# Two chained layers on one Trainium2 core: one constant load moves from ScalarE's queue to GpSimd's, ten start-up products instead of twelve, and batch 1's first products in another order

## The chip, the cores and the metric

The kernel runs on one core of a Trainium2 chip (trn2). A core has TensorE for matmuls, VectorE and ScalarE for elementwise work on SBUF and PSUM, GpSimd for elementwise work on SBUF, and SyncE, which here only issues transfers. ScalarE and GpSimd can issue transfers too, from queues of their own. The metric is the device time of one execution in microseconds; lower is better.

## What is computed

The input `x` has 8 batches of 256 tokens of 128 features; two small id lists choose, per batch, one of 8 experts and one of 4 languages. Cut to what matters:

```python
# layer 0: a per-batch conditioned two-layer net, then 4 rounds of a gated mixture of 4 experts
hidden = relu(x @ wi.T + 2 * (x @ common_a.T) @ common_b.T + 2 * (x @ A[id].T) @ B[id].T)
cond   = the same with wo on hidden, 512 -> 128
for r in range(4):
    cw  = top2_softmax(cur @ Wg[r] + bg[r])
    cur = cur + sum_e cw[e] * (gelu(cur @ W1[e] + b1[e]) @ W2[e] + b2[e])
x = x + cur
# layer 1: a per-batch low-rank product and an embedding, then a gated net with 128 -> 512 -> 512 -> 512 -> 128
x = x + ffn(lowrank(x, lang_id) + emb[lang_id])
```

## The kernel before

The transposed tokens stand in 4 chunks of 512 columns, two batches to a chunk. Every float32 product is made of three single-pass products: operands are split into a high part (`hi`, a cast) and a rest (`lo`, value less its high part), and a product is hi·hi + hi·lo + lo·hi. The change lies in the first 17 us, in the conditioned net.

There each batch has its own weights, one matrix of 128 x 512 for each of two kinds (0: into the hidden layer, 1: out of it). Such a matrix is made in five steps:

1. `merge_group` (TensorE, L543 to L568) multiplies the low-rank factors of a few (batch, kind) pairs, in plain float32, into one PSUM bank each. The factors of a batch are a gather by its id (`first_load`, `lora_load`, L252 to L265): batches 0 and 2 are issued by SP, 1 and 3 by ScalarE, 4 to 7 by SP. `MERGE_GROUPS` has 7 groups; groups 0 and 1 are batches 0 and 1, groups 2 and 3 are batches 2 and 3, group 4 is (4, 0), (5, 0), (4, 1), group 5 is (6, 0), (7, 0), (5, 1).
2. `merged_sum` (VectorE, L1066 to L1075) adds twice the bank to the shared matrix, the base. `base` has two parts, one for each kind, loaded by `base_load(act, 0)` and `base_load(act, 1)`. The sum frees the bank (`merge_free`). The order is `SUMS`: (0,0), (1,0), (0,1), (1,1), (2,0), (3,0), (2,1), (3,1), (4,0), (4,1), (5,0) and so on; the first sum that needs the second base part is the third. Results go to 7 scratch places in turn, so the eleventh sum, of (5,0), waits for the rest of the fourth, (1,1).
3. `merged_high` (ScalarE, L837 to L841) casts the sum to its high part.
4. `merged_low` (GpSimd, L438 to L441) makes the rest. GpSimd does (0,0), (1,0), (0,1), a rest of chunk 1 of x, (2,0), (1,1), and so on.
5. `first_hidden` and `cond_hidden` (TensorE, L581 to L612) multiply x by the weights of kind 0; ScalarE's `relu_high` and VectorE's `relu_low` split the ReLU of that; `cond_out` multiplies it by kind 1.

`first_hidden` serves batch 0: four products with high weights and high x, four with high weights and the rest of x, four with the rest of the weights, and it waits for each operand only where it is first used. `cond_hidden` serves the other batches, three products for each of 4 column blocks in turn, and waits for all operands at its start.

The order of each engine's work is written out by hand, one queue per engine; engines wait on semaphores. TensorE's begins:

```python
            pe.wait_ge(const_done, 1)
            warm(WARM)

            merge_group(0)
            merge_group(1)
            warm(KEEP_WARM)
            merge_group(2)
            merge_group(3)
            first_hidden()
            cond_hidden(1)
            merge_group(4)
            cond_out(0)
            cond_hidden(2)
            merge_group(5)
```

`warm(n)` makes n float32 products of a 128 x 128 tile of zeros that nobody reads, while the first transfers are on their way. A float32 product leaves two records in the trace, a split one leaves one. ScalarE's queue begins with two transfers (base part 0, chunk 0 of x), a table load, the factors of batches 1 and 3, `base_load(act, 1)`, and then `x0_high(0)`, the cast of chunk 0 of x; VectorE's `x0_low(0)` makes its rest. GpSimd's begins with memsets of constants and then goes to `merged_low(0, 0)`.

After this part come 64 steps of the mixture and the last net, matmuls of 512 columns without a gap.

Of the kernel before, what the change touches and what calls it, by code (L numbers as in the profile page):

```python
# [22 lines left out]
P = 128  # L23
BATCHES, SEQ, D = 8, 256, 128
# [33 lines left out]
FFN_PIECES = 3 + 2 * FC  # L58
WARM, KEEP_WARM = 12, 2
RING = 9  # L60
# [51 lines left out]
def adaln_ffn(nc, x_t, batch_ids, cond_base, lora_all, lang_lora, lang_embed,  # L112
              moe_w, vecs, gate_bias, ffn_w, out_t):
    ctx = ExitStack()
    with ctx:
# [311 lines left out]
        def _(pool):  # L427
# [4 lines left out]
            for i in range(EXPERTS):  # L432
# [3 lines left out]
                               pattern=[[-1, EXPERTS], [1, EXPERTS]], channel_multiplier=0).then_inc(const_done, 1)  # L436

            def merged_low(b, kind):  # L438
                pool.wait_ge(mer_hi_done, HIGHS.index((b, kind)) + 1)
                pool.tensor_tensor(mer_lo[:, b % AHEAD, kind, :], merged(b, kind),  # L440
                                   mer_hi[:, b % AHEAD, kind, :].bitcast(F32), ALU.subtract).then_inc(mer_lo_done, 1)  # L441
# [91 lines left out]
        def _(pe):  # L533
# [46 lines left out]

            def first_hidden():  # L581


                hi, lo, cols = mer_hi[:, 0, 0, :], mer_lo[:, 0, 0, :], batch_cols(0)
                pe.wait_ge(mer_hi_done, HIGHS.index((0, 0)) + 1)
                for weights, x in ((hi, xhi), (hi, xlo), (lo, xhi)):
                    if x is xlo:
                        pe.wait_ge(x0_split[0], 1)
                    if weights is lo:
                        pe.wait_ge(mer_lo_done, LOWS.index((0, 0)) + 1)  # L590
                    for f in range(FC):
                        mm = pe.matmul(bank[:, f // 2, (f % 2) * SEQ:(f % 2 + 1) * SEQ], weights[:, f * P:(f + 1) * P],  # L592
                                       x[:, 0, cols], start=weights is hi and x is xhi and f % 2 == 0,
                                       stop=weights is lo, skip_group_check=True)
                mm.then_inc(cond_h_done, 1)

            def cond_hidden(b):
                pe.wait_ge(mer_lo_done, LOWS.index((b, 0)) + 1)
                pe.wait_ge(x0_split[b // PER_CHUNK], 1)
                if b < 2:  # L600
                    free = max(summed_in(2 * b + i, len(MERGED)) for i in range(2))
                    if free:
                        pe.wait_ge(merge_free, free)
                else:
                    pe.wait_ge(relu_lo, b - 1)
                cols = batch_cols(b)
# [114 lines left out]
            merge_group(3)  # L721
            first_hidden()
            cond_hidden(1)
            merge_group(4)
            cond_out(0)
# [108 lines left out]
        def _(act):  # L834
# [113 lines left out]
            lora_load(act, 3)  # L948
            base_load(act, 1)
            x0_high(0)  # L950
# [441 lines left out]
```

## Time and profile before

| | |
|---|---|
| median of 3 runs | 481.35 us (481.15 to 481.97) |
| the profiled execution | 481.35 us |
| its span | 479.6 us |
| TensorE busy | 474.5 us, 99% |
| VectorE, ScalarE, GpSimd busy | 387.1, 393.8, 121.5 us |
| DMA | 27.03 MB, 56 GB/s over the span |

The profile is one execution. Its times are microseconds from the start of the span. Matmul records overlap, since matmuls are pipelined, so a busy TensorE is not TensorE at its peak. A timeline merges instructions of a kind that follow one another (`x24`), and gives the idle time before them and what ended it. A transfer is seen by its issue on the engine's sequencer (`ACTq`, `SPq`, `POOLq`) and the time from there to its landing. `q0` is the software queue (GpSimd's transfers), `q1` and `q10` are hardware queues (SP's and ScalarE's). The tile names are those of the memory: the merged weights lie in `ffn_hi` and `ffn_lo`, the base in `cur`, the factors in `stage`, the sums in `prod`, `stage`, `fifth` and `act_out`.

### The profile page before, as it was taken

The numbers are of one execution on the slowest core, as the hardware profiler recorded it, in microseconds if no ns is written. First come the engines' busy times: TensorE is split into PE (matmuls) and PEld (weight loads), VectorE is DVE, ScalarE is ACT, GpSimd is POOL, SyncE is SP. The second block draws the span as 40 slices with busy tenths as digits, with TensorE's granted clock in tenths as the row PEclk, the third lists the DMA queues.
The fourth block names the chain that finished last, engine by engine and source line by source line (L and its number), as shares of the span: only waits on it lengthen the run. The fifth ranks groups of instructions, "written<-read, shape, count | busy, mean of one in ns | idle before, by whom it ended". The sixth has DMA issues, their size and how long they took to land.

```text
span 479.6 us, 7453 instructions
## 1 busy us (share of the span) xinstructions
PE 474.5 (99%) x2260; PEld 395.0 (82%) x2260; DVE 387.1 (81%) x638; ACT 393.8 (82%) x543; POOL 121.5 (25%) x102
## 2 busy tenths in 40 slices
PE   8999999999999999999999999999999999999997
PEld 7998888888888888888888888888888888888886
DVE  4898999999989898988889898989897759554343
ACT  4889888887889898888888798898888888697643
POOL 3995212121211212122212121171413144400000
PEclk9999999999999999999999999999999999999999
DMA  7604702021120202020202112120202000000002
GB/s 215 211 24 132 287 0 91 2 88 33 57 88 0 88 0 88 0 88 0 88 1 87 44 44 88 44 90 0 88 2 88 2 0 0 1 0 1 0 23 69
DMA packets 8299, 27.03 MB, mean 56 GB/s; under 512 B 2258, under 2 KB 3602, under 8 KB 6098
## 3 DMA queue, kind: packets, MB, share of 16 engines
q1 hardware_dynamic: 7090, 22.45, 13.3%
q0 software_dynamic: 288, 2.88, 1.6%
q10 hardware_dynamic: 896, 1.38, 1.0%
q8 instruction: 14, 0.23, 0.2%
q14 instruction: 11, 0.09, 0.1%
HBM read 25.26 MB, written 1.44 MB: 56 GB/s over the span
## 4 chain that ended last, share of the span: by engine, by line
PE 98%; DMA 1%; SPq 1%; issue 0%; DVE 0%
PE bank L536 34%; PE bank L537 34%; PE bank L540 26%; DMA stage<-lora_all 1%; PE bank L636 1%; PE bank L637 1%; PE bank L561 1%; PE bank L592 0%; PE bank L558 0%; SPq L250 0%; SPq L263 0%; DVE x L1310 0%; SPq L354 0%; SPq L353 0%; SPq L352 0%
## 5 line engine op out<-in xcount | busy, mean ns | idle before, releaser
L857 ACT ACTIVATE act_out<-bank,vec 128x512 f32<-128x512 f32 x256 | 165.1, 682 | 40.5 <-PE bank L540 29.2
L1152 DVE TENSOR_TENSOR hid_lo<-act_out,hid_hi 128x1024 fp32r<-128x1024 f32 x128 | 157.6, 1250 | 32.5 <-ACT hid_hi L862 32.4
L862 ACT ACTIVATE hid_hi<-act_out 128x1024 fp32r<-128x1024 f32 x128 | 135.9, 1062 | 8.0 <-PE bank L540 0.2
L500 POOL TENSOR_TENSOR cur<-cur,prod 128x512 f32<-128x512 f32 x48 | 64.9, 1352 | 233.5 <-DVE prod L1163 233.0
L536 PE MATMUL bank<-hid_hi,moe_hi 128*128 128x512 f32 x256 | 99.8, 390 | 0.0
L540 PE MATMUL bank<-hid_hi,moe_lo 128*128 128x512 f32 x256 | 99.8, 390 | 0.0
L537 PE MATMUL bank<-hid_lo,moe_hi 128*128 128x512 f32 x256 | 99.7, 389 | 0.0
L537 PE MATMUL bank<-xlo,moe_hi 128*128 128x512 f32 x256 | 99.6, 389 | 0.0
L536 PE MATMUL bank<-xhi,moe_hi 128*128 128x512 f32 x256 | 99.6, 389 | 0.0
L540 PE MATMUL bank<-xhi,moe_lo 128*128 128x512 f32 x256 | 99.6, 389 | 0.0
L536 PEld LDWEIGHTS bank<-hid_hi,moe_hi 128*128 128x128 f32 x256 | 48.1, 188 | 11.0
L540 PEld LDWEIGHTS bank<-hid_hi,moe_lo 128*128 128x128 f32 x256 | 48.1, 188 | 10.3
L537 PEld LDWEIGHTS bank<-hid_lo,moe_hi 128*128 128x128 f32 x256 | 48.1, 188 | 10.1
L540 PEld LDWEIGHTS bank<-xhi,moe_lo 128*128 128x128 f32 x256 | 48.1, 188 | 10.1
L537 PEld LDWEIGHTS bank<-xlo,moe_hi 128*128 128x128 f32 x256 | 48.1, 188 | 9.9
L536 PEld LDWEIGHTS bank<-xhi,moe_hi 128*128 128x128 f32 x256 | 48.1, 188 | 9.8
L1163 DVE SCALAR_TENSOR_TENSOR prod<-bank,vec,cw_all 128x512 f32<-128x512 f32 x64 | 47.5, 742 | 0.2 <-PE bank L540 0.2
L536 PE MATMUL bank<-hid_hi,ffn_hi 128*128 128x512 f32 (+1 forms) x108 | 37.8, 353 | 0.1
L537 PE MATMUL bank<-hid_lo,ffn_hi 128*128 128x512 f32 (+1 forms) x108 | 37.4, 350 | 0.0
L1047 ACT ACTIVATE act_out<-bank,vec 128x512 f32<-128x512 f32 x32 | 21.3, 685 | 14.5 <-PE bank L537 14.3
L536 PE MATMUL bank<-xhi,ffn_hi 128*128 128x512 f32 (+1 forms) x80 | 28.3, 353 | 0.0
L537 PE MATMUL bank<-xlo,ffn_hi 128*128 128x512 f32 (+1 forms) x80 | 28.2, 352 | 0.0
(134 smaller groups left out, 570.4 us busy)
## 6 DMA issues: line engine op xcount, KB each, us to landing
cw_all<-cw_dram SPq DMA_DIRECT2D x16, 1024.0 KB, 4.7
stage<-ffn_w POOLq DMA_DIRECT2D x1, 2304.0 KB, 8.6
cw_all<-moe_w SPq DMA_DIRECT2D x4, 512.0 KB, 7.0
stage<-lora_all SPq DMA_DIRECT2D x5, 160.0 KB, 3.9
x<-x_t SPq DMA_DIRECT2D x3, 256.0 KB, 4.0
out_t<-x SPq DMA_DIRECT2D x3, 256.0 KB, 2.5
cur<-cond_base ACTq DMA_DIRECT2D x2, 256.0 KB, 3.4
stage<-ffn_w POOLq DMA_DIRECT2D x1, 512.0 KB, 3.8
```

The lines of the kernel that those rows point to most:

```text
L500: pool.tensor_tensor(cur[:, c, :], cur[:, c, :], prod[:, s % 2, :], ALU.add).then_inc(add_done, 1)
L536: pe.matmul(out, w_hi, r_hi, start=start, stop=False)
L537: mm = pe.matmul(out, w_hi, r_lo, start=False, stop=stop and w_lo is None)
L540: return pe.matmul(out, w_lo, r_hi, start=False, stop=stop)
L561: mm = pe.matmul(bank[:, at, fc * D:(fc + 1) * D], factors[:, fc * P:(fc + 1) * P], factors[:, F:F + D], start=True, stop=True)
L636: pe.matmul(bank[0:SQ, at, :], wg_now[:], xhi[:, c, :], start=True, stop=False)
L637: pe.matmul(bank[0:SQ, at, :], wg_now[:], xlo[:, c, :], start=False, stop=True).then_inc(logit_done, 1)
L857: act.activation(act_out[:, f // 2, f % 2, :], bank[:, f, :], ACT.Gelu_apprx_tanh, bias=vec[:, V_B1 + e * FC + f:V_B1 + e * FC + f + 1]).t ...
L862: act.activation(hid_hi[:, s % 2, 2 * pr:2 * pr + 2, :], act_out[:, pr, :, :], ACT.Copy)\
L1047: act.activation(act_out[:, o // 2, o % 2, :], bank[:, o + FC * (at % 2), :], ACT.Gelu, scale=vec[:, v + o:v + o + 1]).then_inc(gelu_done, 1)
L1152: dve.tensor_tensor(hid_lo[:, s % 2, 2 * pr:2 * pr + 2, :], act_out[:, pr, :, :], hid_hi[:, s % 2, 2 * pr:2 * pr + 2, :].bitcast(F32), ALU ...
L1163: dve.scalar_tensor_tensor(prod[:, s % 2, :], bank[:, 4 + s % 2, :], vec[:, V_B2 + e:V_B2 + e + 1], cw_all[:, c % 2, e, :], ALU.add, ALU.m ...
```

## The change

Three edits, all at the start of the program:

- `base_load(pool, 1)` in GpSimd's queue, behind its constants and a wait until base part 0 has landed, in place of `base_load(act, 1)` in ScalarE's, which stood behind the factors of batch 3.
- `WARM` is 10, not 12.
- `first_hidden` takes the batch as an argument and serves batch 1 too, in place of `cond_hidden(1)`. It waits for the high weights first, and for its two banks (for batch 1, that sums 3 and 4 are done); then for the rest of x and the rest of the weights where they are first used. `cond_hidden` loses the branch for batches under 2.

```diff
--- before.py
+++ after.py
@@ -56,7 +56,7 @@
         1), (6, 1), (7, 1))
 MOE_ORDER = (0, 4, 1, 5, 2, 6, 3, 7)
 FFN_PIECES = 3 + 2 * FC
-WARM, KEEP_WARM = 12, 2
+WARM, KEEP_WARM = 10, 2
 RING = 9
 PREP = 3
 PREP_AT = (2, 6, 10)
@@ -435,6 +435,9 @@
             pool.affine_select(out=upper[:], in_=upper[:], compare_op=ALU.is_gt, fill=0.0, base=0,
                                pattern=[[-1, EXPERTS], [1, EXPERTS]], channel_multiplier=0).then_inc(const_done, 1)
 
+            pool.wait_ge(base_in[0], 16)
+            base_load(pool, 1)
+
             def merged_low(b, kind):
                 pool.wait_ge(mer_hi_done, HIGHS.index((b, kind)) + 1)
                 pool.tensor_tensor(mer_lo[:, b % AHEAD, kind, :], merged(b, kind),
@@ -578,18 +581,21 @@
                     pe.wait_ge(lang_free, 1)
                 logits(c, gate_bank(c))
 
-            def first_hidden():
-
-
-                hi, lo, cols = mer_hi[:, 0, 0, :], mer_lo[:, 0, 0, :], batch_cols(0)
-                pe.wait_ge(mer_hi_done, HIGHS.index((0, 0)) + 1)
+            def first_hidden(b):
+
+
+                hi, lo, cols = mer_hi[:, b, 0, :], mer_lo[:, b, 0, :], batch_cols(b)
+                pe.wait_ge(mer_hi_done, HIGHS.index((b, 0)) + 1)
+                free = max(summed_in(2 * b + i, len(MERGED)) for i in range(2))
+                if free:
+                    pe.wait_ge(merge_free, free)
                 for weights, x in ((hi, xhi), (hi, xlo), (lo, xhi)):
                     if x is xlo:
                         pe.wait_ge(x0_split[0], 1)
                     if weights is lo:
-                        pe.wait_ge(mer_lo_done, LOWS.index((0, 0)) + 1)
+                        pe.wait_ge(mer_lo_done, LOWS.index((b, 0)) + 1)
                     for f in range(FC):
-                        mm = pe.matmul(bank[:, f // 2, (f % 2) * SEQ:(f % 2 + 1) * SEQ], weights[:, f * P:(f + 1) * P],
+                        mm = pe.matmul(bank[:, 2 * b + f // 2, (f % 2) * SEQ:(f % 2 + 1) * SEQ], weights[:, f * P:(f + 1) * P],
                                        x[:, 0, cols], start=weights is hi and x is xhi and f % 2 == 0,
                                        stop=weights is lo, skip_group_check=True)
                 mm.then_inc(cond_h_done, 1)
@@ -597,12 +603,7 @@
             def cond_hidden(b):
                 pe.wait_ge(mer_lo_done, LOWS.index((b, 0)) + 1)
                 pe.wait_ge(x0_split[b // PER_CHUNK], 1)
-                if b < 2:
-                    free = max(summed_in(2 * b + i, len(MERGED)) for i in range(2))
-                    if free:
-                        pe.wait_ge(merge_free, free)
-                else:
-                    pe.wait_ge(relu_lo, b - 1)
+                pe.wait_ge(relu_lo, b - 1)
                 cols = batch_cols(b)
                 for f in range(FC):
                     w = slice(f * P, (f + 1) * P)
@@ -719,8 +720,8 @@
             warm(KEEP_WARM)
             merge_group(2)
             merge_group(3)
-            first_hidden()
-            cond_hidden(1)
+            first_hidden(0)
+            first_hidden(1)
             merge_group(4)
             cond_out(0)
             cond_hidden(2)
@@ -946,7 +947,6 @@
             act.wait_ge(ids_in, 16)
             first_load(act, 1)
             lora_load(act, 3)
-            base_load(act, 1)
             x0_high(0)
             merged_high(0, 0)
             merged_high(1, 0)
```

On TensorE, behind the fourth group of merges, the products of batches 0 and 1 into the hidden layer. Before:

```order
L592 MATMUL bank<-xhi,ffn_hi 128x256 [waits mer_hi_done]
L592 MATMUL bank<-xhi,ffn_hi 128x256 x3
L592 MATMUL bank<-xlo,ffn_hi 128x256 [waits x0_split0]
L592 MATMUL bank<-xlo,ffn_hi 128x256 x3
L592 MATMUL bank<-xhi,ffn_lo 128x256 [waits mer_lo_done]
L592 MATMUL bank<-xhi,ffn_lo 128x256 x3
L536 MATMUL bank<-xhi,ffn_hi 128x256 [waits merge_free,x0_split0,mer_lo_done]
L537 MATMUL bank<-xlo,ffn_hi 128x256
L540 MATMUL bank<-xhi,ffn_lo 128x256
```

Now:

```order
L598 MATMUL bank<-xhi,ffn_hi 128x256 [waits mer_hi_done]
L598 MATMUL bank<-xhi,ffn_hi 128x256 x3
L598 MATMUL bank<-xlo,ffn_hi 128x256 [waits x0_split0]
L598 MATMUL bank<-xlo,ffn_hi 128x256 x3
L598 MATMUL bank<-xhi,ffn_lo 128x256 [waits mer_lo_done]
L598 MATMUL bank<-xhi,ffn_lo 128x256 x3
L598 MATMUL bank<-xhi,ffn_hi 128x256 [waits merge_free,mer_hi_done]
L598 MATMUL bank<-xhi,ffn_hi 128x256 x3
L598 MATMUL bank<-xlo,ffn_hi 128x256 [waits x0_split0]
L598 MATMUL bank<-xlo,ffn_hi 128x256 x3
L598 MATMUL bank<-xhi,ffn_lo 128x256 [waits mer_lo_done]
L598 MATMUL bank<-xhi,ffn_lo 128x256 x3
```

Batch 1's twelve products stand in the order of batch 0's, and the wait for the rest of its weights (`mer_lo_done`) stands before the ninth of them instead of the first.

On ScalarE, the end of its transfers and its first casts (`prod` holds the first two sums). Before:

```order
L250 ISA x2
L253 ISA
L253 DMA stage<-lora_all 64x640
L271 DMA cur<-cond_base 128x512
L925 ACTIVATE xhi<-x 128x512 [waits x_in0]
L840 ACTIVATE ffn_hi<-prod 128x512 [waits merge_free] x2
```

Now:

```order
L250 ISA x2
L253 ISA
L253 DMA stage<-lora_all 64x640
L926 ACTIVATE xhi<-x 128x512 [waits x_in0]
L841 ACTIVATE ffn_hi<-prod 128x512 [waits merge_free] x2
```

The second base part is gone from between the factors of batch 3 and the cast of x.

On GpSimd, the end of its constants and its first rests. Before:

```order
L433 MEMSET need 32x1 x4
L435 ISA
L435 AFFINE_SELECT upper<-upper 32x16 [waits const_done]
L440 TENSOR_TENSOR ffn_lo<-prod,ffn_hi 128x512 [waits mer_hi_done] x2
L440 TENSOR_TENSOR ffn_lo<-stage,ffn_hi 128x512 [waits mer_hi_done]
```

Now:

```order
L433 MEMSET need 32x1 x4
L435 ISA
L435 AFFINE_SELECT upper<-upper 32x16 [waits const_done]
L271 DMA cur<-cond_base 128x512 [waits base_in0]
L443 TENSOR_TENSOR ffn_lo<-prod,ffn_hi 128x512 [waits mer_hi_done] x2
L443 TENSOR_TENSOR ffn_lo<-stage,ffn_hi 128x512 [waits mer_hi_done]
```

The load stands there with its wait for the first part, ahead of the first rest.

## Rows read from the trace of the kernel before

**Rows 1.** The page, part 1: busy us, share of the span, instructions.

```profile
PE 474.5 (99%) x2260; PEld 395.0 (82%) x2260; DVE 387.1 (81%) x638; ACT 393.8 (82%) x543; POOL 121.5 (25%) x102
```

**Rows 2.** Waits of TensorE, whole span: us in total, times, longest us.

```profile
PE bank L632 <- POOL blank L428: 1.1, 1, 1.1
PE bank L558 <- DMA stage<-lora_all: 0.8, 1, 0.8
```

**Rows 3.** The chain of waits, 0 to 25 us: start us, us, what.

```profile
3.09 0.35 SPq L263
...
4.72 3.95 DMA stage<-lora_all
```

**Rows 4.** Timeline of TensorE: start us, us, what [idle before <-releaser].

```profile
1.06 5.09 PE L632 MATMUL bank<-blank 128*128 128x128 f32 x24 [1.06 <-POOL blank L428]
6.08 0.70 PE L558 MATMUL bank<-stage 32*128 32x512 f32 x2
...
7.18 0.71 PE L632 MATMUL bank<-blank 128*128 128x128 f32 x4
8.71 0.70 PE L558 MATMUL bank<-stage 32*128 32x512 f32 x2 [0.81 <-DMA stage<-lora_all]
...
9.91 0.74 PE L592 MATMUL bank<-xhi,ffn_hi 128*128 128x256 f32 x4
...
12.97 0.70 PE L558 MATMUL bank<-stage 32*128 32x512 f32 x2
...
14.09 0.36 PE L536 MATMUL bank<-hid_hi,ffn_hi 128*128 128x256 f32 x1
...
17.15 0.70 PE L558 MATMUL bank<-stage 32*128 32x512 f32 x2
```

**Rows 5.** Timeline of VectorE, 4 to 18 us.

```profile
5.37 0.18 DVE L1242 CAST wg_now<-wg 128x32 fp32r<-128x32 f32 x1
6.42 0.69 DVE L1064 TENSOR_TENSOR xlo<-x,xhi 128x512 fp32r<-128x512 f32 x1 [0.86 <-ACT xhi L925]
7.32 1.29 DVE L1074 SCALAR_TENSOR_TENSOR prod<-bank,cur 128x512 f32<-128x512 f32 x2 [0.21 <-PE bank L561]
9.18 1.29 DVE L1074 SCALAR_TENSOR_TENSOR stage<-bank,cur 128x512 f32<-128x512 f32 x2 [0.57 <-DMA cur<-cond_base]
...
12.18 0.68 DVE L1074 SCALAR_TENSOR_TENSOR prod<-bank,cur 128x512 f32<-128x512 f32 x1
...
16.40 0.69 DVE L1074 SCALAR_TENSOR_TENSOR stage<-bank,cur 128x512 f32<-128x512 f32 x1 [0.99 <-POOL ffn_lo L440]
```

**Rows 6.** Timeline of ScalarE, 5 to 18 us.

```profile
5.11 0.59 ACTq L271 DMA_DIRECT2D cur<-cond_base  x1
5.75 0.63 ACT L925 ACTIVATE xhi<-x 128x512 fp32r<-128x512 f32 x1 [2.53 <-issue]
```

**Rows 7.** Timeline of GpSimd, 8 to 18 us.

```profile
8.75 2.54 POOL L440 TENSOR_TENSOR ffn_lo<-prod,ffn_hi 128x512 fp32r<-128x512 f32 x2 [6.45 <-ACT ffn_hi L840]
...
15.01 1.29 POOL L440 TENSOR_TENSOR ffn_lo<-stage,ffn_hi 128x512 fp32r<-128x512 f32 x1
```

**Rows 8.** DMA issues at 0.8, 3.1, 5.1 and 306.1 us: KB, us to landing.

```profile
cur<-cond_base ACTq DMA_DIRECT2D x1, 256.0 KB, 2.8
...
stage<-lora_all SPq DMA_DIRECT2D x1, 80.0 KB, 2.2
...
cur<-cond_base ACTq DMA_DIRECT2D x1, 256.0 KB, 4.0
...
stage<-ffn_w POOLq DMA_DIRECT2D x1, 512.0 KB, 3.8
```

**Rows 9.** Windows: engines' busy us, TensorE's clock, DMA share, GB/s.

```profile
5.25:5.75 0.50, 0.50 (x5) 0.50 (x4) 0.27 (x2) 0.00 (x0) 0.00 (x0) 1.00 0.03 10
...
6.75:8.75 2.00, 1.19 (x20) 0.88 (x12) 1.64 (x3) 0.71 (x2) 0.00 (x0) 1.00 1.06 288
```

**Rows 10.** The zeros' line, 0 to 9 us: ns min/median/max.

```profile
L632 PE MATMUL bank<-blank x28: 274/421/582, 1.1 to 7.6; 128*128 128x128 f32 x28
```

## The prediction

> **What bounds the kernel now.** I read the page first: TensorE is busy for 99% of the span [rows 1]. The list of waits for TensorE comes next: over the whole 479.6 us it names one wait behind the start, 0.8 us for a transfer of factors [rows 2]. So from about 9 us on the kernel is a stream of matmuls with no hole that a view names, and an edit in the first 17 us is worth exactly what it moves that stream forward; nothing else in the diff reaches further. The chain of waits says what ends last before the stream: the factors of batch 2, issued by SP at 4.72, landed 3.95 later, at 8.67 [rows 3], and TensorE's third group of merges starts at 8.71 [rows 4].
>
> The timelines of the other engines show two more chains that are almost as late. **VectorE**: it sums batches 0 and 1 of the first kind from 7.32, then waits 0.57 us for the second part of the base (issued by ScalarE at 5.11, landed 4.0 later) and sums without a pause from 9.18 to 12.86 [rows 5, 6, 8]. The eighth sum frees a bank for TensorE's merges of batches 4 and 5 at 12.97: 0.11 behind it. **GpSimd**: it starts at 8.75, when ScalarE has written the first high weights, and its rests follow one another without a pause up to 16.30 [rows 7]; VectorE waited 0.99 us for that one to make its eleventh sum, 16.40 to 17.09 [rows 5], and TensorE's next merges start at 17.15 [rows 4].
>
> **The change part by part.** All times below are those of the profiled execution, 481.35 us, which is also the median of the three runs (481.15 to 481.97); 1.75 us of it lie around the span.
>
> *Ten products of zeros.* A product leaves two records; 24 records take 5.09 us, 0.21 each, at a record's length of 421 ns. The four records at 7.18 take 0.71 with the last one's own 0.27, so 0.44 for two products [rows 4, 10]. By the one rate the first merges would start 0.85 earlier (5.23), by the other 0.44 earlier (5.64), from 6.08. The factors of batch 0 are there at 3.09 + 2.2 = 5.29 [rows 3, 8], so 0.79 is the most. I take 5.6 (0.48 earlier): the merges right behind the zeros have the same 0.70 us per pair of records as those at 8.71, so the last zeros ran at the higher of the two levels (2.4 GHz) and are cheap ones to lose.
>
> *The second base part leaves ScalarE.* Its issue held ScalarE from 5.11 to 5.70, and the split of x starts at 5.75, its wait put down to "issue" [rows 6]. It now starts at about 5.16, and VectorE's rest of x moves from 6.42 to 5.82 and ends at 6.5. This is worth nothing alone, since VectorE then waited 0.21 us for TensorE; but without it the end of that rest at 7.11 would stop the gain of the zeros after 0.21 us [rows 5].
>
> *First sum.* It follows the first merges: 7.32 less 0.48 is 6.84 (bounds 6.53, where VectorE gets free, and 6.88). ScalarE's high weights and GpSimd's first rest follow directly: 8.75 becomes 8.27.
>
> *The second base part on GpSimd.* It waits for the first part, landed at 0.8 + 2.8 = 3.6 [rows 8]. Queued behind this wait is only the first rest at 8.27, so the wait and the issue itself cost nothing. Landing: the nearest row is the 512 KB load by GpSimd, 3.8 from its issue [rows 8]; that with some 0.6 for wake-up and issue (the same size as ScalarE's 0.59) gives 8.0 as the late end; ScalarE's own 2.8 for 256 KB from 3.6 gives 6.4 as the early end. I take 7.1: half the bytes of the 3.8, and DMA engines that are all but idle from 5.25 to 5.75 (share 0.03) [rows 9]. VectorE wants it for its third sum at 6.84 + 2 x 0.6 = 8.04 (0.6 each, as the five from 9.18 to 12.18), so its wait of 0.57 is gone by either end, and sums 3 and 4 start 1.1 earlier.
>
> *What the queues gain.* From 6.75 to 8.75 the DMA engines are full (share 1.06, 288 GB/s) [rows 9]; taking 256 KB out is worth at most 0.9 us there, and nothing if the software queue's bytes still run then. I take 0.65: factors of batch 2 at 8.0, merges at 8.05. Sums 5 to 8 end at about 11.7, so the bank is free before TensorE is there (12.97 less 0.66: 12.3). But the output of batch 0, at 14.09, waits for ReLU and its rest of the first hidden products, which move by the 0.66 of the merges only; so TensorE's branch is 0.66 early from there.
>
> *High weights first in batch 1.* The same 12 products, same columns, bank pair and weight loads: no cost (both batches' 24 take 3.06, from 9.91 to 12.97 [rows 4]). Its wait for the low weights of batch 1 moves 8 products, about 1 us, back. GpSimd has them at 11.29 - 0.48 = 10.81, TensorE would have asked 12 products of 0.13 behind 9.91 - 0.66, at 10.8; so it saves at most 0.1, and that is hidden by the next step.
>
> *The sum.* The merges at 17.15 have two feeders. TensorE alone: the 24 products behind 14.09 take the 3.06 of the 24 from 9.91, so it is itself there at 17.15 at the latest, less 0.66 is 16.49. GpSimd's chain: 16.30 - 0.48 = 15.82, VectorE's sum and 0.16 of hand-overs behind it: 16.67. The later one decides: 17.15 - 16.67 = **0.48 us**. Behind it VectorE, ScalarE and GpSimd follow TensorE, and no landing ends a wait of TensorE there [rows 2]. 481.35 - 0.48 = **480.9 us**, 0.1%, which is under the 0.2% (0.96 us) that a measurement of this kernel can tell from no change.
>
> A rule speaks against the new place of the transfer. VectorE runs small copies and casts up to 5.55, the last of them at 5.37 [rows 5], and the descriptors of the base part would be written from about 4.2. The Trainium skill ("DMA: Bandwidth & Descriptors", section SWDGE vs HWDGE vs iDMA) says that descriptor rings of GpSimd's DMAs are SBUF state from which VectorE in a two-port mode locks GpSimd out, while ScalarE's and SP's DMAs are immune. By that rule the first rival below comes true (481.3); no row before shows a GpSimd DMA beside such copies.
>
> **The rivals.**
> 1. *GpSimd's transfer comes no earlier.* If its descriptors stay behind until VectorE's copies end at 5.55, it lands 3.2 to 3.8 later, 8.8 to 9.3, where it landed before (9.1). The third sum then stays at about 9.2, the eighth ends at 12.9 and the merges of batches 4 and 5 stay at 12.97. GpSimd's chain still comes 0.48 earlier, but TensorE's own stream to 17.15 moves by no more than the 0.1 of its hand-over there: gain 0 to 0.1, 481.3 us. For it: the first DMA of that queue in the program. Against: the queue was idle and the issue is early by half a microsecond. Chance 0.12.
> 2. *Slower, by TensorE's clock.* Before, zeros are in flight until 6.15, and records shorten from 421 to 274 ns only near their end [rows 4, 10]. Now they end at 5.5, and the first merges wait if the factors of batch 0 slip behind the base's bytes past 5.5 (0.2 of slack). If TensorE then stands still at the moment at which it had been raised, merges 0 and 1 run at 1.2 GHz, 2.3 us in place of 1.15 (6.08 to the zeros at 7.18 [rows 4], 1.1): first sum at 7.9 in place of 7.32, 0.6 later; if it lasts through the third merges and 24 hidden products (3 us more), up to 3.5. Time 482.0 to 484.9, 482.5 as the likely one; from a loss of 0.96 on it counts as slower. Against: 10 products are still 4.4 us of work without a hole. Chance 0.1.
> 3. *More than I count.* TensorE's branch alone could give the 0.9 of the queues and 0.1 of hand-over, 1.0, 480.3 us, if GpSimd's chain were not the bound, that is if the first merges started at 5.3 (chain 0.79 early) and other rests had slack the profiled execution doesn't show. Chance 0.1.
> The forecast has 0.68.
>
> **How the numbers follow.** The forecast's own bounds are 0.44 to 0.79: 480.6 to 480.9; with the 0.3 by which runs of one kernel differ, 480.3 to 481.2. To hold 8 in 10 the range takes in rival 1 and the upper part of the run spread: 480.2 to 481.9. Left out: most of rival 2 and the far end of 3. Faster by over 0.2% (under 480.4) is rival 3 and the low edge of the forecast: 0.15. Slower by over 0.2% (over 482.3) is the larger part of rival 2: 0.07. Within: 0.78.
>
> **What would show it.** Right: zeros end near 5.5; first merges at 5.6; ScalarE's split of x at 5.2; base part on the software queue, landed by 8.0; VectorE without a pause from 6.84 to about 9.3; GpSimd's first rest near 8.3; third merges near 8.05; merges of batches 4 and 5 near 12.3; the merges now at 17.15 near 16.7, still released by VectorE behind GpSimd; a span near 479.1. Wrong: a base landing behind 8.1, a first rest of GpSimd that doesn't move, merges 0 and 1 longer than 1.1 us, or a wait of TensorE behind 17 us.

## The result, and the profile of the changed kernel

Slower, by more than the bound: 483.85 us, median of 22 runs (481.95 to 485.34), against 481.62 (481.08 to 483.80, 22 runs) of the kernel before on the same chips; ratio 1.0044, interval 1.0034 to 1.0054. That is 2.2 us more, where 0.5 less was forecast, and outside the range (480.2 to 481.9). The profiled execution is the longest of the 22, 485.34, with a span of 483.6. It shows both effects named below in full, not the typical case.

The page's first and second parts (40 slices of 12 us):

```profile
span 483.6 us, 7445 instructions
...
PE 477.2 (99%) x2256; PEld 397.4 (82%) x2256; DVE 387.7 (80%) x638; ACT 393.9 (81%) x543; POOL 121.9 (25%) x103
...
PEclk8899999999999999999999999999999999999999
```

TensorE is busy 2.7 us longer than in [rows 1], with four records fewer, and the clock row holds an 8 in the first two slices; in the page of before it is 9 everywhere. The waits of TensorE over the whole span, and then the chain of waits up to 18 us (start us, us, what):

```profile
PE bank L561 <- DMA stage<-lora_all: 2.1, 2, 1.9
PE bank L633 <- POOL blank L428: 1.1, 1, 1.1
```

```profile
4.72 5.25 DMA stage<-lora_all
...
10.02 0.66 PE bank L561
...
12.21 4.96 PE bank L598 x24
```

The one wait of [rows 2] grew from 0.8 to 1.9 us, with 0.2 more ahead of the first merges. In the chain, the factors of batch 2, issued by SP at 4.72 as before, land 5.25 later, not 3.95 [rows 3]. The timeline of TensorE:

```profile
1.06 4.64 PE L633 MATMUL bank<-blank 128*128 128x128 f32 x20 [1.06 <-POOL blank L428]
5.92 0.83 PE L561 MATMUL bank<-stage 32*128 32x512 f32 x2 [0.22 <-DMA stage<-lora_all]
...
7.38 0.71 PE L633 MATMUL bank<-blank 128*128 128x128 f32 x4
10.02 1.22 PE L561 MATMUL bank<-stage 32*128 32x512 f32 x2 [1.93 <-DMA stage<-lora_all]
...
12.13 1.22 PE L598 MATMUL bank<-xhi,ffn_hi 128*128 128x256 f32 x4
13.15 1.05 PE L598 MATMUL bank<-xlo,ffn_hi 128*128 128x256 f32 x4
...
16.54 0.63 PE L598 MATMUL bank<-xhi,ffn_lo 128*128 128x256 f32 x4
17.10 0.70 PE L561 MATMUL bank<-stage 32*128 32x512 f32 x2
```

The third merges start at 10.02 instead of 8.71, and two things behind them are longer without a wait in between: the merges of groups 2 and 3 take 2.11 us (10.02 to 12.13; before 1.20), the 24 products behind them 4.97 (12.13 to 17.10; before 3.06) [rows 4]. 1.31 + 0.91 + 1.91 is 4.13; TensorE's last matmul of the program starts at 480.11, before at 476.11, so all of the 4.0 us is in these three, and 0.13 comes back behind them. The windows of that stretch, in the columns of [rows 9], first of the changed kernel, then of the kernel before over the same work:

```profile
6.00:7.92 1.92, 1.92 (x24) 1.77 (x24) 1.59 (x6) 0.00 (x0) 0.00 (x0) 1.00 0.92 255
7.92:10.01 2.09, 0.17 (x2) 0.00 (x0) 1.86 (x4) 1.99 (x4) 1.27 (x2) 0.92 1.07 224
10.02:12.10 2.08, 2.08 (x20) 1.89 (x20) 0.00 (x0) 1.05 (x2) 2.08 (x2) 0.50 1.01 253
12.13:16.40 4.27, 4.27 (x22) 4.27 (x21) 2.72 (x5) 1.30 (x2) 1.59 (x2) 0.50 0.87 244
17.10:18.20 1.10, 1.10 (x14) 0.98 (x13) 0.28 (x1) 1.10 (x3) 1.10 (x2) 1.00 0.95 272
```

```profile
8.71:9.90 1.19, 1.19 (x20) 1.08 (x20) 0.72 (x2) 0.56 (x1) 1.15 (x1) 1.00 1.09 317
9.91:12.97 3.06, 3.06 (x26) 2.93 (x24) 3.06 (x6) 3.06 (x5) 3.06 (x4) 1.00 0.88 253
```

The granted clock is 1.00 up to the hole, 0.92 over the hole, 0.50 in both stretches behind it (1.2 GHz), and 1.00 again from 17.1; before it is 1.00 throughout. (The row also says 1.00 for the first 5 us, where the zeros take 421 ns a record as at the lower level: it counts that level only behind the first rise, which the trace puts at 6.24 here and at 5.60 before.) So the profile holds two effects: a later landing (1.3), and a clock that fell to the lower level while TensorE stood still (2.8). The other engines, in this order: VectorE, ScalarE, GpSimd.

```profile
5.57 0.18 DVE L1234 COPY wg_raw<-vec 128x16 f32<-128x16 f32 x1 [5.57 <-DMA gbias<-gate_bias]
...
7.29 1.29 DVE L1074 SCALAR_TENSOR_TENSOR prod<-bank,cur 128x512 f32<-128x512 f32 x2 [0.26 <-PE bank L561]
8.50 1.28 DVE L1074 SCALAR_TENSOR_TENSOR stage<-bank,cur 128x512 f32<-128x512 f32 x2
12.12 0.69 DVE L1074 SCALAR_TENSOR_TENSOR fifth<-bank,cur 128x512 f32<-128x512 f32 x1 [2.34 <-PE bank L564]
```

```profile
5.28 0.63 ACT L926 ACTIVATE xhi<-x 128x512 fp32r<-128x512 f32 x1 [2.06 <-DMA x<-x_t]
```

```profile
3.92 0.86 POOL L271 DMA_DIRECT2D cur<-cond_base  x1 [1.61 <-DMA cur<-cond_base]
8.74 2.51 POOL L443 TENSOR_TENSOR ffn_lo<-prod,ffn_hi 128x512 fp32r<-128x512 f32 x2 [3.96 <-ACT ffn_hi L841]
```

VectorE's sums 3 and 4 no longer wait for the base (8.50 instead of 9.18, [rows 5]), and then it idles 2.34 us for TensorE, where before it went on at once. Last, the transfers issued from 3.85, 4.4 and 4.7 us, and the queues' share from 5.25 to 7.25 (packets, MB, share of 16 engines):

```profile
cur<-cond_base POOLq DMA_DIRECT2D x1, 256.0 KB, 4.5
stage<-lora_all ACTq DMA_DIRECT2D x1, 160.0 KB, 4.6
stage<-lora_all SPq DMA_DIRECT2D x1, 160.0 KB, 5.3
```

```profile
q0 software_dynamic: 76, 0.26, 44.7%
q10 hardware_dynamic: 61, 0.13, 20.6%
q1 hardware_dynamic: 29, 0.06, 10.2%
```

The load is issued early (3.9) and lands at 8.47. 76 of its 80 packets run on the software queue between 5.25 and 7.25, the first at 5.5, and in that time only 0.06 MB of SP's queue and 0.13 of ScalarE's do; before those two moved 0.15 and 0.20. Both factor loads behind it are late: 4.6 instead of 3.2 us for batch 3, 5.3 instead of 3.9 for batch 2.

### The profile page after: what moved, and what is told of

Read it like the earlier page. It is cut to its first block, busy times and chain, and to the rows that moved or that the text cites. A ratio compares the mean times of both kernels' runs of the same rounds, so it can differ in the third digit from the quotient of the medians.

```text
span 483.6 us, 7445 instructions
## 1 busy us (share of the span) xinstructions
PE 477.2 (99%) x2256; PEld 397.4 (82%) x2256; DVE 387.7 (80%) x638; ACT 393.9 (81%) x543; POOL 121.9 (25%) x103
## 4 chain that ended last, share of the span: by engine, by line
PE 97%; DMA 1%; SPq 1%; issue 0%; DVE 0%
PE bank L539 34%; PE bank L540 34%; PE bank L543 26%; DMA stage<-lora_all 1%; PE bank L598 1%; PE bank L637 1%; PE bank L564 1%; PE bank L638 1%; PE bank L561 0%; SPq L250 0%; SPq L263 0%; DVE x L1310 0%; SPq L354 0%; SPq L353 0%; SPq L352 0%
## 5 line engine op out<-in xcount | busy, mean ns | idle before, releaser
L539 PE MATMUL bank<-xhi,ffn_hi 128*128 128x512 f32 (+1 forms) x76 | 27.1, 357 | 0.0
L540 PE MATMUL bank<-xlo,ffn_hi 128*128 128x512 f32 (+1 forms) x76 | 27.0, 356 | 0.0
```

The lines of the kernel that those rows point to most:

```text
L539: pe.matmul(out, w_hi, r_hi, start=start, stop=False)
L540: mm = pe.matmul(out, w_hi, r_lo, start=False, stop=stop and w_lo is None)
```

## The experiments

Each kernel ran beside the kernel before. e1 to e4 ran side by side and share its runs, as do e5 to e8, e9 to e12, and e13 with e14. The expectations set two theories of the late landing against each other: the **place** (P), 256 KB ahead of the factors of batches 2 and 3 whatever queue carries them, and the **software queue** (S), GpSimd's queue as such slows the others. The **clock** is the third cause, in part of the executions. Each execution reports the mean granted clock of its span. Where a trace shows one stretch of 3.41 us at the lower level (e5, e10), the mean is 0.995 or 0.996; with 6.83 us (changed, e9) it is 0.993; with none between the first merges and the last, 0.997 to 1.000. That counts the falls in executions without a trace, with one exception. The mean also holds the time behind the last matmul, where the level falls too: in e14's trace there are 2.9 us of it, with no fall before, and the mean is 0.997. So in e14, whose executions spread from 0.990 to 1.000 without a gap, the count is not one of falls.

| kernel | zeros | base part 1 | median us (n) | ratio, interval | mean clock 0.996 or less | median of the others |
|---|---|---|---|---|---|---|
| changed | 10 | GpSimd | 483.85 (22) | 1.0044, 1.0034 to 1.0054 | 16 of 22 | 482.71 |
| e9, changed again | 10 | GpSimd | 484.21 (5) | 1.0058, 1.0045 to 1.0071 | 4 of 5 | 484.21 |
| e3 | 12 | GpSimd | 482.47 (12) | 1.0022, 1.0007 to 1.0038 | 1 of 12 | 482.29 |
| e10, e3 again | 12 | GpSimd | 482.62 (7) | 1.0032, 1.0018 to 1.0046 | 3 of 7 | 482.36 |
| e2, old order | 12 | GpSimd | 482.75 (12) | 1.0034, 1.0021 to 1.0046 | 4 of 12 | 482.43 |
| e4, 4 more later | 10 | GpSimd | 482.56 (11) | 1.0021, 1.0010 to 1.0032 | 0 of 11 | 482.56 |
| e13 | 14 | GpSimd | 482.81 (12) | 1.0007, 0.9977 to 1.0037 | 3 of 12 | 482.59 |
| e14 | 8 | GpSimd | 484.75 (12) | 1.0062, 1.0037 to 1.0087 | 5 of 12 (not all falls) | 484.57 |
| e5, old order | 12 | ScalarE, early | 483.70 (12) | 1.0026, 1.0001 to 1.0051 | 6 of 12 | 482.53 |
| e6, old order | 12 | half on GpSimd | 482.08 (12) | 1.0003, 0.9983 to 1.0024 | 0 of 12 | 482.08 |
| e1, old order | 10 | ScalarE | 481.39 (12) | 0.9998, 0.9976 to 1.0021 | 0 of 12 | 481.39 |
| e7 | 10 | ScalarE | 481.10 (12) | 0.9990, 0.9969 to 1.0011 | 0 of 12 | 481.10 |
| e12, e7 again | 10 | ScalarE | 481.63 (11) | 1.0002, 0.9993 to 1.0010 | 0 of 11 | 481.63 |
| e8, 2 more later | 10 | ScalarE | 481.37 (12) | 0.9986, 0.9962 to 1.0010 | 0 of 12 | 481.37 |
| e11, 2 fewer later | 12 | ScalarE | 481.48 (12) | 1.0008, 0.9994 to 1.0022 | 0 of 12 | 481.48 |

The kernel before beside them: 481.67 (35 runs) for e1 to e4, 481.61 (35) for e5 to e8, 481.42 (24) for e9 to e12, 481.71 (23) for e13 and e14; in those 117 runs three had 0.996 or less (487.18 to 487.65). Nine more lay above 483, up to 485.47, at 0.999 or 1.000, and so did three runs of e1 and one of e11, at 0.998 or more: there is another source of long runs, which no view explains. A ratio compares runs taken next to each other and isn't the quotient of two medians.

**e1_zeros_only: the zeros alone.** In the kernel before:

```diff
-WARM, KEEP_WARM = 12, 2
+WARM, KEEP_WARM = 10, 2
```

> The kernel before with ten products of zeros, nothing else changed. Theory Z (the two products less let the clock fall: TensorE stands still around the moment of the rise and does too little until the third merges): median 483 to 484, the granted clock falls to 0.5 for some us in the first 17, in the profile or in the mean clock of the runs (under 0.999). Theory B (the base part's bytes ahead of the factors of batches 2 and 3 make the hole that lets the clock fall): within 0.2 of the kernel before or up to 0.4 faster, clock 1.0 from about 5.6 on, third merges at 8.7 as before.

No difference, and no fall in 12 executions, so the zeros alone do not make the loss. The first merges started at 5.63 in its trace, as forecast; the third (8.32) followed their factors, which no product of zeros moves, and TensorE's last matmul started at 475.96, 0.15 before that of the kernel before.

**e2_base_only: the load alone.** In the kernel before:

```diff
+            pool.wait_ge(base_in[0], 16)
+            base_load(pool, 1)
...
-            base_load(act, 1)
```

> The kernel before with the second base part issued by GpSimd behind the first part's landing, twelve zeros, old order in batch 1. Theory B: factors of batch 2 land at 9.5 or later where they landed at 8.67, third merges at 9.5 to 10, the clock falls in some executions, median 482.5 to 484. Theory Z: within 0.3 of the kernel before, clock 1.0 from the first rise on, even if the factors land later by some tenths.

The timeline of TensorE and the transfers issued by 4.7 us:

```profile
6.23 0.70 PE L561 MATMUL bank<-stage 32*128 32x512 f32 x2
...
9.84 0.70 PE L561 MATMUL bank<-stage 32*128 32x512 f32 x2 [1.79 <-DMA stage<-lora_all]
...
11.04 0.74 PE L595 MATMUL bank<-xhi,ffn_hi 128*128 128x256 f32 x4
```

```profile
stage<-lora_all ACTq DMA_DIRECT2D x1, 160.0 KB, 4.5
stage<-lora_all SPq DMA_DIRECT2D x1, 160.0 KB, 5.1
```

This edit alone is slower, 1.0034, with the third merges at 9.84 behind a wait of 1.79 us, and the clock on the upper level in this execution: groups 2 and 3 take 1.20 and the hidden products the old time. Its last matmul starts at 477.10, 1.0 behind before's. So the late landing is the load's, not the zeros' or the order's. In the traces of all eight kernels with the whole load on GpSimd the factors of batch 2 land between 9.46 and 10.27 and those of batch 3 between 8.59 and 9.31; in the six with the load in its old place they land between 8.10 and 8.67, and 7.28 and 7.74. The groups don't touch.

**e3_all_but_zeros: the change with 12 zeros.** In the changed kernel:

```diff
-WARM, KEEP_WARM = 10, 2
+WARM, KEEP_WARM = 12, 2
```

> The changed kernel with twelve zeros. Theory Z: 481 to 481.5, the clock does not fall. Theory B: 482.5 to 484, as in the run with the base part alone, less at most 0.1 for the order. If both are needed (ZB): this, the zeros alone and the base part alone are each within 0.5 of the kernel before, and only all together cost 2 us.

Still slower, 482.47 against 481.67, with the third merges at 10.13 in its trace. But 1 of 12 executions had a fallen clock, and 16 of 22 in the changed kernel, which did not run beside it; e9 and e10 repeat the pair side by side.

**e4_keep_six: the change, with four more products of zeros in the hole.** In the changed kernel:

```diff
-WARM, KEEP_WARM = 10, 2
+WARM, KEEP_WARM = 10, 6
```

> The changed kernel with six products of zeros instead of two between the second and third groups of merges (four more, eight records, about 0.9 us). Any theory in which the clock falls because TensorE does nothing from 7.9 until the factors of batch 2 land: the zeros fill 0.9 us of that hole, the clock stays up, median back to 480.8 to 481.6. If the fall does not come from that hole, or the hole is only the sign of late factors that cost by themselves: 483 to 484 as the changed kernel.

The timeline of TensorE:

```profile
7.05 1.60 PE L633 MATMUL bank<-blank 128*128 128x128 f32 x12
9.57 0.70 PE L561 MATMUL bank<-stage 32*128 32x512 f32 x2 [0.91 <-DMA stage<-lora_all]
...
10.77 0.73 PE L598 MATMUL bank<-xhi,ffn_hi 128*128 128x256 f32 x4
```

The eight added records fill half of the hole, the third merges still wait for their factors (9.57), and none of 11 executions fell. The median, 482.56, is in neither theory's range: without a fall the late factors still cost 0.9. That the four products prevent the fall isn't shown by this run alone, since e3 beside it fell only once.

**e5_scalar_ahead and e6_half_by_gpsimd: place against queue.**

In the kernel before, for e5:

```diff
+            base_load(act, 1)
             lora_load(act, 3)
-            base_load(act, 1)
```

And for e6, where `base_half(queue, half)` loads 256 of the 512 columns, each half with its own semaphore:

```diff
+            pool.wait_ge(base_in[0], 16)
+            base_half(pool, 0)
...
-            base_load(act, 1)
+            base_half(act, 1)
```

> The kernel before, with the second base part issued by ScalarE ahead of the factors of batch 3 instead of behind them: the same place in line as with GpSimd, but on the hardware queue. Theory P (what costs is the place: 256 KB in front of the factors of batches 2 and 3): factors of batch 2 land at 9.3 to 9.8, third merges as late, median 482.3 to 483. Theory S (what costs is the software queue itself, its packets or its spread over the DMA engines): factors of batch 2 land at 8.5 to 9.0, median within 0.4 of the kernel before; the base part lands at 7.5 with its 16 shares within 0.5 us of one another.

> The kernel before, with the left half of the second base part (128 KB) issued by GpSimd behind the first part's landing and the right half by ScalarE in the old place. Theory P: half of what the whole costs, factors of batch 2 at 9.1 to 9.3, median 482.0 to 482.3. Theory S with a cost per packet: the same half. Theory S with a cost of the queue as such: as late as with the whole, 9.5 to 9.8, median 482.5 to 483.

The base load of e5, issued at 3.80, its factors of batches 2 and 3, issued at 4.72 and 4.98, the queues' share from 5.25 to 7.25, and its TensorE timeline:

```profile
cur<-cond_base ACTq DMA_DIRECT2D x1, 256.0 KB, 4.4
...
stage<-lora_all SPq DMA_DIRECT2D x1, 160.0 KB, 3.9
stage<-lora_all ACTq DMA_DIRECT2D x1, 160.0 KB, 5.3
```

```profile
q10 hardware_dynamic: 162, 0.30, 53.2%
q1 hardware_dynamic: 70, 0.14, 28.0%
```

```profile
8.14 0.71 PE L632 MATMUL bank<-blank 128*128 128x128 f32 x4
10.43 0.70 PE L558 MATMUL bank<-stage 32*128 32x512 f32 x2 [1.57 <-DMA stage<-lora_all]
...
12.06 1.22 PE L592 MATMUL bank<-xhi,ffn_hi 128*128 128x256 f32 x4
```

In e5 no byte of the program's start is on the software queue. The load, ahead of batch 3's factors on ScalarE's hardware queue, takes 4.4 us (GpSimd's took 4.5), and the third merges start at 10.43; the clock fell in this execution too, so groups 2 and 3 take 1.63. The executions without a fall have a median of 482.53, as e2's 482.43. But the way there is another one, and neither theory forecast it. The merges wait for the factors of both batches. In e5 those of batch 2, on SP's queue, land at 8.63, as before (8.67) and as theory S had it, and SP's queue moves 0.14 MB from 5.25 to 7.25, as before (0.15). The late ones are batch 3's, behind the load in ScalarE's own queue and issued 0.5 later: 10.29, before 7.74. With GpSimd's load both are late, and SP's queue moves 0.03 to 0.07 MB in that time in all eight traces. So 256 KB ahead of the factors cost about the same by either queue, as theory P has it for the time; but only the load on GpSimd's queue held back SP's queue. Whether that is its bytes or the software queue as such, e5 doesn't tell.

Half of the bytes (e6) cost 0.47 in the median, with an interval that holds no change, and 0.4 in the lowest run (481.40 against 481.00). Its profiled execution was its fastest. There the 128 KB on GpSimd's queue delayed no factors (batch 2 at 8.35, third merges at 8.39, forecast 9.1 to 9.8 by every theory), and TensorE waited elsewhere, 0.47 us ahead of the merges of group 4 for VectorE's sums, which had waited for the right half (landed 9.39). So the price isn't shown to go by bytes.

**e7_zeros_order, its repeat e12, and e8: the change without the load.** In the changed kernel as below; e8 is e7 with two more products of zeros behind the first merges (`KEEP_WARM` 4).

```diff
-            pool.wait_ge(base_in[0], 16)
-            base_load(pool, 1)
...
+            base_load(act, 1)
```

> The changed kernel with the second base part back on ScalarE: ten zeros and batch 1's new order alone. If the base part's move is the only harm: median 480.9 to 481.4, faster than the kernel before by 0.2 to 0.6, factors of batch 2 at 8.3 to 8.7. If the ten zeros alone let the clock fall in a share of executions: a second group of times near 483 to 485, larger than with twelve (4 of 35 over 483.3 in the kernel before).

> As the one before, with four zeros instead of two between the second and third groups of merges (0.44 us more work, done before the factors of batch 2 land). If the upper group of times comes from the hole ahead of the third merges: it gets rarer, median 480.9 to 481.3 and the slowest run under 483. If not: the same spread as the run before.

> Ten zeros and batch 1's new order with the second base part on ScalarE, again, since its first interval reached past 1. Median 480.9 to 481.4, 0.2 to 0.5 under the kernel before, with fewer times over 483 than it; or the same as before within 0.2, if the first run's gain was chance.

The timeline of TensorE in e7:

```profile
5.38 0.70 PE L558 MATMUL bank<-stage 32*128 32x512 f32 x2
...
8.52 0.70 PE L558 MATMUL bank<-stage 32*128 32x512 f32 x2 [0.84 <-DMA stage<-lora_all]
...
9.72 0.74 PE L595 MATMUL bank<-xhi,ffn_hi 128*128 128x256 f32 x4
...
17.03 0.70 PE L558 MATMUL bank<-stage 32*128 32x512 f32 x2
```

With the load back in its place the hole is 0.84 again and nothing fell in the 35 executions of the three. In e8 the two added products fill the hole: its third merges, at 8.52, wait for nothing. e7's median was 0.5 under before's; its repeat's was 0.2 above. Both intervals hold 1, so zeros and order together are worth nothing that a run can show. The last matmul of e7's profile starts at 475.90, 0.2 earlier.

**e9_changed_again, e10_twelve_zeros_again, e11_before_keep_none.** The first two repeat the changed kernel and e3 side by side. e11 is the kernel before without zeros behind the first merges:

```diff
-WARM, KEEP_WARM = 12, 2
+WARM, KEEP_WARM = 12, 0
```

> The changed kernel as it is, in one call with the next run, so that the two differ in the zeros alone. Theory C (two causes: the base part's bytes cost 1.1 to 1.4 in every execution, and with ten zeros the clock then falls in most executions): most times over 483.2, a few at 482.0 to 482.8, median 483.5 to 484. Theory N (the zeros don't matter; the times over 483.2 depend on the chip or the hour): the same share of times over 483.2 here as in the next run.

> The changed kernel with twelve zeros, again. Theory C: nearly all times at 481.9 to 483.1, median 482.3 to 482.7. Theory N: as the run before it.

> The kernel before without the two products of zeros between the second and third groups of merges, all transfers as before. The hole ahead of the third merges begins 0.45 us earlier (7.25 instead of 7.7) and ends with the factors as before, at 8.7: 1.4 us. If a hole of TensorE is what lets the clock fall, even with nothing late: a larger share of times over 483 than the kernel before has (it has 4 in 35), median 481.5 to 483.5. If only a hole of 2 us does it: as the kernel before, within 0.3.

Two windows of e10, in the columns of [rows 9]:

```profile
10.40:13.70 3.30, 3.30 (x27) 3.08 (x22) 1.74 (x3) 1.19 (x3) 3.30 (x4) 0.50 0.98 262
15.00:16.00 1.00, 1.00 (x12) 0.86 (x11) 0.38 (x1) 1.00 (x2) 0.00 (x0) 1.00 0.85 258
```

e9 repeated the result: 1.0058, with the third merges at 10.31 in its trace and 6.83 us at the lower level. e10's profiled execution fell as well, for 3.41 us: the clock row is 0.50 from 10.4 to 13.7 and 1.00 from 15.0, where the changed kernel's was still 0.50. Against e3 the share of falls was larger, 3 of 7, where theory C forecast nearly none. Together 12 zeros fell 4 times in 19 and 10 zeros 20 times in 27, but side by side it is 3 of 7 against 4 of 5, which is too few to tell, so theory N isn't ruled out for the size of the difference. 12 zeros are not safe in any case: e2 fell 4 times in 12, and e5 6 times. In e11 TensorE waited 0.70 us ahead of the third merges, no longer than before's 0.81, since its factors had landed at 8.1 in the profiled execution. No execution fell, and the median didn't move (481.48 against 481.42): where the factors come on time, no run shows a use of the zeros behind the first merges. It doesn't tell what a long hole does with 12 zeros and the old place; only the moved load made one.

**e13_fourteen_zeros, e14_eight_zeros: more and fewer zeros.** In the changed kernel, for e13 (e14 has 8):

```diff
-WARM, KEEP_WARM = 10, 2
+WARM, KEEP_WARM = 14, 2
```

> The changed kernel with fourteen zeros: TensorE works without a hole to 6.95, merges 0 and 1 start 0.8 later than with ten standing still behind them, the two zeros behind them end near 8.7, so the hole ahead of the third merges is 1.3 us instead of 2.1. If the share of falls follows the work done ahead of that hole: falls in at most one in ten executions, median 482.0 to 482.6. If it is set by something else than TensorE's work: a share as with ten or twelve.

> The changed kernel with eight zeros: they end at 4.6 and TensorE stands still to 5.9, where the first merges start as with ten; the hole ahead of the third merges is the same 2.1 us. If a hole ahead of the first merges is what makes ten zeros worse than twelve: falls in nearly all executions, median 483.9 to 485.5, some over 486. If only the second hole counts: as with ten, median 483.5 to 484.3.

14 zeros fell 3 times in 12, not one in ten, with 482.59 for the others, and the wait ahead of the third merges was 0.72 us in its trace. The interval holds no change; the kernel before had two runs of 487 beside it. 8 zeros were the slowest, 1.0062, but not by falls alone: all 12 were long, also the seven over 0.996 (483.45 to 486.69). Its profiled execution (483.45, no fall, third merges at 9.50) had its last matmul at 476.76, and 5.1 us between that and the end of the span, where the kernel before has 3.5. That is 1.6 of its 2.1 us, spent behind the last matmul, and why is open; e14 is no evidence on the clock.

## Why the prediction was wrong, step by step

- **"What the queues gain": failed, and it decided the sign.** The step had the factors of batch 2 at 8.0, from 8.67, with bounds of 0 and 0.9 of gain. It took 256 KB out of the full stretch from 6.75 to 8.75 and never asked what those bytes do in the stretch they move to. Before, the load was issued at 5.11, behind batches 3's and 2's factors, and it landed behind theirs, at 9.15. At 3.9 it is ahead of both, and no row had shown what a load on GpSimd's queue does to the others. The idle DMA engines that [rows 9] show from 5.25 to 5.75 were a hole of 0.5 us ahead of a full stretch; at that stretch's 288 GB/s it holds 0.14 MB of the 0.26. The factors came at 9.97 here, 9.79 in e2. The missing bound on the side of a loss stood in the same rows: 256 KB at 288 GB/s is 0.9 us, and the third merges came 0.8 (e14) to 1.4 (e3) later than the 8.71 of before in the traces that stayed on the upper clock, on both sides of that. (In the six traces with the load in its old place they start from 8.14 to 8.71, so 8.71 is the late end.) In time the moved load costs 0.6 to 1.1 us: the executions without a fall of the changed kernel, e2, e3, e4, e5, e10 and e13 (482.29 to 482.71) against the kernel before beside each. (e9 has only one such, 484.21.)
- The Trainium skill ("DMA: Bandwidth & Descriptors", section Issuing engines are not separate DMA queues) says that transfers of every issuing engine end up on the same 16 DMA engines and interleave there. The traces agree for GpSimd's load: while its 0.25 MB moved, SP's queue moved 0.05 in e2, 0.15 before. In e5, with as many bytes ahead on ScalarE's queue, SP's load was not delayed (3.9 us, as before), so that bytes interleave doesn't by itself say whose load is late. It would have been the rule to weigh, in place of the one on descriptor rings.
- **Rival 2, the clock: its mechanism came true, in another place.** It was given 0.1, 482.0 to 484.9. Its slip of batch 0's factors was real (landed 5.88, 5.29 forecast, with 0.22 of idle time), but not the load's doing, since they landed at 5.93 in e8, with the load in its old place; and the merges 0 and 1 were not the price. The clock was raised during them in this execution (6.24), and fell in the hole ahead of the *third* merges: its 0.92 over the 2.09 us up to 10.01 is 0.35 us at the lower level. A mean clock of 0.994 to 0.996 goes with 1.1 us more in the changed kernel (483.85, 12 executions, against 482.71), 1.4 in e2 (483.86 against 482.43) and 1.7 in e5 (484.27 against 482.53); 0.992 to 0.993 with 2.6 (485.30, 4 executions). Since 16 of 22 executions fell, the median contains it: of the 2.2 us, about 1.1 are the moved load and 1.1 the fall. With four products more in the hole (e4), none of 11 fell. In e10 and e5 the level fell only behind the wait, at 10.34 and 11.13, with TensorE at work again since 10.08 and 10.43. The Trainium skill ("TensorE: Matmul & The Clock Gate", section HAM oscillation — how this bites in real kernels) describes TensorE's clock falling again while it waits for a transfer, with waits of about 3 to 5 us in its example; the 0.50 behind the wait of 1.93 us agrees with the fall, and shows it behind a shorter wait.
- **Zeros: right in their place, too large in the sum.** Forecast 5.6 for the first merges; e1 and e7 had them at 5.63 and 5.38. But without a gain at the third merges TensorE's own stream decides, and the last matmul came 0.11 to 0.21 earlier in e1, e7, e8 and e12, not 0.48. The times can't tell (e1: 0.9976 to 1.0021). With the load moved, the two missing products go with more falls, 20 of 27 against 4 of 19, though mostly not side by side. If that is their doing, costing them by their own length alone was a second error there.
- **The load leaves ScalarE: right.** The split of x started at 5.28 (5.16 forecast), bound by the landing of x and no longer by the issue.
- **First sum and GpSimd's first rest: wrong by size.** 7.29 and 8.74 against 6.84 and 8.27. The first merges started at 5.92, not 5.6, held by their factors, and took 1.46 us to the zeros at 7.38 (1.10 before), the first 0.3 of it ahead of the rise of the clock.
- **The landing of the base: wrong by size.** 8.47, forecast 7.1, bounds 6.4 to 8.0; the base stood beside the factors, 4.5 us for 256 KB where I took less than the 3.8 of 512 KB. VectorE wanted it at 8.50, so it cost nothing.
- **Rival 1: not it.** The load's first packet moved at 5.49, ahead of VectorE's first small copy (5.57). The other traces try it: the first packet came at 5.4 to 5.5 in all eight, whether the copies ran from 4.67 to 5.53 (e10) or only from 6.20 (e13). So these copies held nothing back; whether they are in the two-port mode that the rule speaks of no view says.
- **High weights first in batch 1: right, as nothing.** e2 to e3 is 482.75 to 482.47 side by side, and each ratio lies in the other's interval.
- **The sum's two feeders** held in e7: the merges of group 5 at 17.03 (17.15 before), released behind GpSimd. In the changed kernel they start at 21.26, 4.1 later, and without a wait.

Open: whether the load on GpSimd's queue delays SP's factors by its bytes or by its queue; a load of 256 KB on SP's queue, or one on GpSimd's behind the factors, was not run. Open too: why 10 zeros fell so much more often than 12. In the traces they differ ahead of the first merges alone (0.2 us of idle time), while the moment at which the clock is raised lay anywhere, with no order by the number of zeros (with the load moved: 5.08 with 14, 5.88 to 6.92 with 12, 4.95 to 6.30 with 10, 4.51 with 8). One order does show: of the eight traces with the load on GpSimd, the three that fell have the latest rises (6.24, 6.30, 6.92), the five others 4.51 to 5.90. e5 doesn't fit it, with a rise at 4.30 and a fall. No version beat the kernel before by more than its interval.

## What to carry to other kernels

A transfer moved forward in a full start-up is moved ahead of somebody: list what is issued within a microsecond behind its new place on every queue, price the delay as its bytes over the rate of the full stretch, and ask whether one of those is what the critical engine waits for. That is a rough size of the loss and no more: it came out at 0.8 to 1.4 us for 0.9 here, and at nothing for half of the bytes in e6's trace. Read each queue's landings before saying which transfer was late: e2 and e5 took the same time by different ones. A wait of TensorE early in the program costs more than its length where the clock falls in it or behind it; here four products in the hole went with no fall in 11 executions, and two saved ahead of it gained nothing that a run shows. The granted clock of every run, not of the profiled one alone, tells wait and fall apart.

## What the runs showed of the hardware that I had not expected

- GpSimd's load was issued 0.3 us behind its releaser (landing at 3.6, issue record at 3.92, 0.86 us long), its first packet moved at 5.49, and it landed 4.5 us (e2 4.7) behind its issue, more than twice the 512 KB row's time per byte [rows 8]. The same bytes by ScalarE's queue, issued at 3.80, took 4.4.
- While GpSimd's 256 KB moved (5.25 to 7.25), SP's queue moved 0.03 to 0.07 MB in eight traces; without them, 0.12 to 0.19 in six, and 0.14 in e5, with the same bytes early on ScalarE's queue.
- In every trace with a fall the lower level lasted 3.41 or 6.83 us, and the wait ahead of the third merges was 1.57 to 2.25 us (e5, e10, changed, e9). e2, e3 and e14 waited 1.71 to 1.94 us too, and their profiled executions stayed on the upper level: such a hole can go without a fall.
- The clock was raised at different moments in executions of one kernel: 5.88 and 6.92 us in e3 and its repeat e10, 4.94 and 6.41 in e7 and its repeat e12.
